# Splitting the context term of a recommendation tower into high and low halves on stacked rows: two fp32 passes replaced by one fp32r pass

## What is computed

```
def _cin_layer(X0, Xi, W, b):
    Wr = W.reshape(H, F0_, Fi)
    return jnp.einsum('hjk,bjd,bkd->bhd', Wr, X0, Xi) + b[None, :, None]
...
z = concatenate([X1.sum(2), X2.sum(2), X3.sum(2)], axis=1)       # 512 x 384
h = jnp.concatenate([z, dense_ctx], axis=1)                      # 512 x 400
h = jnp.maximum(h @ W_top1 + b_top1, 0.0)                        # 400 x 512
h = jnp.maximum(h @ W_top2 + b_top2, 0.0)                        # 512 x 256
y = h @ W_top3
```

## Time and profile before

| | |
|---|---|
| median of 3 runs | 665.23 us (664.14 to 666.54) |
| the profiled execution's own time | 665.45 us |
| its span | 663.6 us |
| PE busy | 648.5 us (98%) |
| DVE busy | 558.7 us (84%) |
| ACT busy | 440.8 us (66%) |
| POOL busy | 468.5 us (71%) |
| granted TensorE clock, mean | 0.992 of full speed |

### The profile page before, as it was taken

The page is one execution under the profiler, slowest core; times in us unless marked ns, Lnnn a source line. Parts: engine busy times, 40 slices in busy tenths (PEclk is TensorE's granted clock), DMA queues, the critical chain, the costliest instruction groups (busy, mean ns, idle before and its releaser), DMA issues.

```text
span 663.6 us, 11303 instructions
## 1 busy us (share of the span) xinstructions
PE 648.5 (98%) x3070; PEld 518.3 (78%) x3070; DVE 558.7 (84%) x1558; ACT 440.8 (66%) x1449; POOL 468.5 (71%) x376
## 2 busy tenths in 40 slices
PE   7998999999999999999999999999999999999997
PEld 7785678777788777777778877778778887777877
DVE  4669899999984799999995699999997589999970
ACT  3554667677763777777773677877785477778761
POOL 6888888888873688888875478787876367444540
PEclk8899999999999999999999999999999999999999
DMA  6013474140403004040311301313040300400000
GB/s 216 14 36 107 130 243 128 23 120 8 128 10 114 16 8 128 6 122 16 94 44 45 90 5 46 91 29 108 18 121 15 107 17 8 126 2 5 1 1 1
DMA packets 38357, 42.25 MB, mean 64 GB/s; under 512 B 17824, under 2 KB 22549, under 8 KB 38166
## 3 DMA queue, kind: packets, MB, share of 16 engines
q1 hardware_dynamic: 32661, 40.23, 19.9%
q0 software_dynamic: 5632, 1.31, 2.2%
HBM read 8.84 MB, written 0.00 MB: 13 GB/s over the span
## 4 chain that ended last, share of the span: by engine, by line
PE 92%; DVE 2%; DMA 2%; ACT 1%; issue 1%; POOL 1%; SPq 0%; POOLq 0%; DVEq 0%
PE p_u L804 22%; PE p_u L806 21%; PE p_u L805 21%; PE p_x L779 6%; PE p_tower L827 5%; PE p_g L818 5%; PE p_x L776 2%; PE p_x L774 2%; PE p_x L773 2%; PE p_tower L854 1%; DMA g_all<-w_in 1%; PE p_x L744 1%; DVE parts L636 1%; DVE z L595 1%; PE p_x L756 1%
## 5 line engine op out<-in xcount | busy, mean ns | idle before, releaser
L457 ACT ACTIVATE prod<-p_u,x0t 128x128 f32<-128x128 f32 x1024 | 290.4, 376 | 101.5 <-PE p_u L806 101.4
L636 DVE SCALAR_TENSOR_TENSOR parts<-p_u,x0t,parts 128x128 f32<-128x128 f32 x1024 | 283.4, 341 | 41.3 <-PE p_u L806 41.2
L804 PE MATMUL p_u<-w1h,x1h 128*128 128x512 f32 (+1 forms) x640 | 288.4, 451 | 1.0 <-ACT x1h L438 1.0
L806 PE MATMUL p_u<-w1h,x1l 128*128 128x512 f32 (+1 forms) x640 | 250.2, 391 | 0.0
L805 PE MATMUL p_u<-w1l,x1h 128*128 128x512 f32 (+1 forms) x640 | 250.1, 391 | 0.0
L335 POOL DMA_INDIRECT emb<-table_in,idx_all x176 | 207.9, 1181 | 49.9 <-issue 47.5
L354 POOL TENSOR_TENSOR parts<-parts,prod 128x512 f32<-128x512 f32 x128 | 176.2, 1377 | 51.7 <-ACT prod L457 38.3
L804 PEld LDWEIGHTS p_u<-w1h,x1h 128*128 128x128 f32 x640 | 120.9, 189 | 37.9 <-issue 8.6
L805 PEld LDWEIGHTS p_u<-w1l,x1h 128*128 128x128 f32 x640 | 121.5, 190 | 35.6 <-issue 10.8
L806 PEld LDWEIGHTS p_u<-w1h,x1l 128*128 128x128 f32 x640 | 120.7, 189 | 26.1
L349 POOL TENSOR_TENSOR parts<-prod 128x512 f32<-128x512 f32 x64 | 83.3, 1301 | 73.0 <-ACT prod L457 72.2
(11 more groups left out here) (86 smaller groups left out, 388.2 us busy)
## 6 DMA issues: line engine op xcount, KB each, us to landing
fac_b<-xx SPq DMA_DIRECT2D x90, 234.0 KB
fac_a<-xx SPq DMA_DIRECT2D x45, 78.0 KB
emb<-table_in,idx_all POOLq DMA_INDIRECT x176, 3.2
g_all<-w_in SPq DMA_DIRECT2D x3, 832.0 KB, 6.2
w<-w_in SPq DMA_DIRECT2D x1, 2496.0 KB, 9.2
xx<-xx SPq DMA_DIRECT2D x30, 78.0 KB
fac_b<-xx SPq DMA_DIRECT2D x15, 156.0 KB
bd<-x0t SPq DMA_DIRECT2D x120, 10.0 KB
```

Of the source, the lines that this page charges most:

```text
L457: last = nc.scalar.activation(dst[:, i * H:(i + 1) * H], u[:, i * H:(i + 1) * H], ACT.Copy, scale=x0t[:, par, t, j:j + 1])
L636: nc.vector.scalar_tensor_tensor(out=chain[i][:, p], in0=u[:, i * H:(i + 1) * H], scalar=x0t[:, par, t, j:j + 1], in1=add, op0=ALU.mult, o ...
L804: nc.tensor.matmul(u, xh, wh, start=True, stop=False)
L806: nc.tensor.matmul(u, xl, wh, start=False, stop=True).then_inc(u_full, 1)
```

## The change

The two context operands become fp32r tensors of 112 rows (`CTX_ROWS = 96 + CTX`). Rows 0, 32, 64 and 96 onward hold 16 rows each: for the weights `wt1c` high, high, low, low, and for the factors `ctxt` high, low, high, low. One matmul over the 112 rows then sums all four products of the halves; the rows between are zeros.

The raw fp32 rows are loaded elsewhere: the weights into `y_rows` (the row `y`, made 16 rows high) and the context into the first 16 rows of `h1`, which the tower first writes later. The four high halves are written by ACT (`context_high_half`) and the four low halves by DVE (`context_low_half`), 16 rows by 512 columns each, in slots 5, 7, 9 and 11 of macro batch 4 (`S_CTX`, `M == MACROS`). The low halves 0 and 2 wait for the high half of the same slot; 1 and 3 need only that of the slot before last. POOL is untouched; SP issues the same DMAs with one wait fewer, to other places.

```
+CTX_ROWS = 96 + CTX
+S_CTX = [5, 7, 9, 11]
+CTX_HIGH = [0, 32, 0, 64]
+CTX_LOW = [64, 96, 32, 96]
...
-        wt1c = sb("wt1c", [128, TOP1])
+        wt1c = sb("wt1c", [CTX_ROWS, TOP1], FP32R)
-        ctxt = sb("ctxt", [128, B])
+        ctxt = sb("ctxt", [CTX_ROWS, B], FP32R)
...
-        y = sb("y", [1, B])
+        y_rows = sb("y_rows", [CTX, B])
+        y = y_rows[0:1, :]
+        wt1c_raw = y_rows[:]
+        ctxt_raw = h1[0:CTX, :, :].rearrange("p c b -> p (c b)")
...
-                sp.wait_ge(context_cleared, 2)
-                sp.dma_start(wt1c[0:CTX, :], wt1_d[3 * 128:3 * 128 + CTX, :]).then_inc(tower_in, 16)
+                sp.dma_start(wt1c_raw, wt1_d[3 * 128:3 * 128 + CTX, :]).then_inc(context_in, 16)
...
+            def context_high_half(i):
+                raw, half = (wt1c_raw, wt1c) if i < 2 else (ctxt_raw, ctxt)
+                act.wait_ge(context_in, 16 * (2 + STACK))
+                act.wait_ge(context_cleared, 2)
+                nc.scalar.activation(half[CTX_HIGH[i]:CTX_HIGH[i] + CTX, :], raw, ACT.Copy).then_inc(context_high, 1)
...
             def tower_h1(n, p_h1):
                 act.wait_ge(h1_full, n + 1)
+                act.wait_ge(context_low, 4)
...
+                        if M == MACROS and s in S_CTX:
+                            context_high_half(S_CTX.index(s))
...
+            def context_low_half(i):
+                raw, half = (wt1c_raw, wt1c) if i < 2 else (ctxt_raw, ctxt)
+                high = 0
+                dve.wait_ge(context_high, 2 * (i // 2) + 1)
+                dve.wait_ge(context_in, 16 * (2 + STACK))
+                nc.vector.tensor_tensor(out=half[CTX_LOW[i]:CTX_LOW[i] + CTX, :], in0=raw,
+                                        in1=half[high:high + CTX, :].bitcast(FP32), op=ALU.subtract
+                                        ).then_inc(context_low, 1)
...
+                        if M == MACROS and s in S_CTX:
+                            context_low_half(S_CTX.index(s))
...
-                pe.wait_ge(tower_in, 16 * (4 + STACK))
+                pe.wait_ge(tower_in, 16 * 2)
+                pe.wait_ge(context_high, 4)
+                pe.wait_ge(context_low, 4)
```

More of the change, by code:

```diff
@@ L172, in build @@
         context_cleared = sem("context_cleared")
+        context_in = sem("context_in")
+        context_high = sem("context_high")
+        context_low = sem("context_low")
         idx_made = sem("idx_made")
@@ L292, in load_tower @@
                     n, at = FIRST_SAMPLES[c], GATHERS * c
-                    sp.dma_start(ctxt[0:CTX, c:MACRO_B:STACK], ctx_d[:, at:at + n], allow_slow_non_contiguous=True).then_inc(tower_in, 16)
-                sp.dma_start(ctxt[0:CTX, MACRO_B:B], ctx_d[:, MACRO_B:B]).then_inc(tower_in, 16)
+                    sp.dma_start(ctxt_raw[:, c:MACRO_B:STACK], ctx_d[:, at:at + n], allow_slow_non_contiguous=True).then_inc(context_in, 16)
+                sp.dma_start(ctxt_raw[:, MACRO_B:B], ctx_d[:, MACRO_B:B]).then_inc(context_in, 16)
             def body(n, has_prev, has_next):
@@ L692, in _ @@
             nc.vector.memset(bd[:], 0.0).then_inc(bd_cleared, 1)
-            nc.vector.memset(wt1c[:], 0.0).then_inc(context_cleared, 1)
-            nc.vector.memset(ctxt[:], 0.0).then_inc(context_cleared, 1)
+            nc.vector.memset(wt1c[:].bitcast(FP32), 0.0).then_inc(context_cleared, 1)
+            nc.vector.memset(ctxt[:].bitcast(FP32), 0.0).then_inc(context_cleared, 1)
             dve.wait_ge(w0_in, 16)
```

## The result

The changed kernel takes 671.56 us (median of 7 runs, 670.32 to 673.46) against 666.54 us (7 runs, 664.14 to 669.77) of the kernel before beside it: ratio 1.0088, 95% interval 1.0062 to 1.0114. It is slower, by 5.0 us in the medians and 5.9 us by the ratio, more than twice the 2.49 us that were forecast. The span of the profiled execution grew from 663.6 to 669.6 us.

What follows compares the result with a forecast made beforehand. PE bounds the kernel (busy 648.5 of 663.6 us), with a chain through a full DVE in macro batch 4. Delay 3.83 us minus 1.34 us gained gives +2.49 us: 667.7 us forecast against the median 665.23 us, range 665.3 to 669.3 us.

Steps and rivals of the forecast that it cites:

- the cost term of the sum: Macro batch 4: ACT's copy into g_all and PE's start of `tower_z3` come 3.30 + 0.53 = 3.83 us later.
- DVE is full ahead of the product of group 2: Macro batch 4, from slot 4 on: DVE runs back to back, first idle 0.93 us in slot 15.
- the chain behind it: Macro batch 4: product of group 2, z0h, quad, copy, `tower_z3`; any delay moves PE by its full length.
- The first low half waits for ACT, 0.41 us.: Slot 5 of macro batch 4: DVE, ready at 185.28 us, waits until 185.69 us for ACT's high half.
- Three low halves at 0.60 us, the fourth high half at 0.53 us.: Macro batch 4: DVE's three before the product add 1.80 us; ACT's one between z0h and slot 12's quad adds 0.53 us.
- POOL's collisions, 1.09 us.: Macro batch 4: POOL's additions lengthen the first two low halves by 0.72 and 0.37 us; the third meets none.
- The short pass costs one record.: Context matmuls of the towers: each single pass takes 0.112 us, not 0.223; twelve on the path gain 1.34 us.
- The bound of 0.06 us a pass: Context matmuls: fastest case for a short pass of 128 columns, raising the gain of twelve to 1.96 us.
- The 81 ns per matmul: Context matmuls: the skill's figure for 128 columns, giving 1.70 us gain; the prediction kept the trace's 0.112 us instead.
- The last block's passes give nothing.: Tail: its four short passes gain nothing, since PE waits 0.96 us for DVE's fold anyway.
- The prediction is wrong if `tower_z3` starts before 195 us.: Refuting sign in slot 15 of macro batch 4: PE's `tower_z3` starting before 195 us, against 192.26 us before the change.
- Or if PE is idle anywhere else that it was not: Refuting sign: new PE idle time outside the forecast waits, about 3.8 us in slots 10 to 15 of macro batch 4.

Runs made afterwards that it cites:

- e1: Changed kernel with all eight conversions in slots 15, 17, 19 and 21 of macro batch 4, not 5, 7, 9 and 11: 665.25 us, ratio 0.9997.
- e6: Changed kernel with only DVE's four low halves moved to slots 15, 17, 19 and 21, ACT's high halves left in place: 665.12 us, ratio 0.9993.
- e4: Changed kernel plus eight unread fp32r matmuls of 512 columns on PE before `tower_z3`'s wait in slot 15 of macro batch 4: 668.05 us, ratio 1.0052.
- e5: Changed kernel with DVE's low halves written to rows 0 to 15 of an unused tensor, products with low halves left out: ratio 1.0071.
- e11: Changed kernel plus eight unread fp32r matmuls before the slot 15 wait and five unread fp32 ones in the tail: 667.99 us, ratio 1.0029.

## Why the prediction was wrong

**The step that failed** is the cost term of the sum: "The copy, and PE's start of `tower_z3`, come 3.30 + 0.53 = 3.83 us later", taken as the whole cost. The delay itself was 4.56 us, and PE's clock behind the waits, of which the prediction has no word and which it thus put at nothing, cost another 1.54 us in macro batch 4 and 1.63 us in the tail of the profiled execution. The mechanism, its place and its sign were right. Point by point:

- *DVE is full ahead of the product of group 2 and the chain behind it has no slack.* Right: e1 moves the operations 10 slots on and the loss is gone, e6 splits it into DVE's part and ACT's.
- *The first low half waits for ACT, 0.41 us.* Near: 184.96 - 0.08 us, when DVE would have gone on, to 185.22 us, 0.34 us.
- *Three low halves at 0.60 us, the fourth high half at 0.53 us.* The durations were right (0.71 us for the third low half, which meets no addition of POOL, and 0.63 us), the distances too small: 0.11 us on each side of a low half, some 0.6 us for the three, and 0.12 us on each side of the high half. I took the distance from operations that keep their partitions and overlooked that these move 16 rows from partition 0 to 32, 64 or 96. The Trainium skill says it (VectorE: DVE Perf Modes, Two Vector instructions with no wait between them): an instruction whose output starts in another group of 32 partitions than the last output into the same memory did starts only when every earlier one has finished. The trace agrees for DVE (0.03 us behind the end, where 0.08 us ahead of it is usual), and shows the same on ACT, of which the page does not speak.
- *POOL's collisions, 1.09 us.* Right: 0.54 and 0.55 us behind POOL's end, on the first and the second low half, none on the third; 0.76 + 0.27 = 1.03 us.
- Together the chain was **4.6 us and not 3.83 us** (4.56 us by the start of `tower_z3`, 4.60 us by e4): 0.34 for the wait, 1.80, 1.03 for POOL, 0.6 for the holds on DVE, and 0.77 for the high half.
- *The short pass costs one record.* Right: 0.47 us for four of them, 1.41 us for twelve, where 1.34 us were forecast. The bound of 0.06 us a pass was not reached. The 81 ns per matmul of the Trainium skill (TensorE: Matmul & The Clock Gate, Back-to-back issue gap) would have given an estimated 1.70 us, which the trace does not show.
- *The last block's passes give nothing.* Worse: they lengthened PE's wait in the tail from 0.96 to 1.47 us, and the 1.63 us that were lost at half clock behind it were in no sum. That part is chance in half of the cases: e4, e5 and e6 have the same wait in their profiles and keep the clock.
- *The clock.* **1.54 us** in macro batch 4 (e4) and **1.63 us** in the tail of the profiled execution were missing. The forecast with the true chain, 4.6 - 1.4 = +3.2 us, would have been inside the range; the two stretches at 1.2 GHz carried the result out of it. The prediction had PE idle for 3.8 us between slots 10 and 15 (3.93 us measured) and priced only the idling. The trace of the kernel before has a warning that no row of the prediction shows: PE waits 1.22 and 0.54 us between 7.9 and 10.2 us, and from about 12 to 22 us it runs at half clock. The second of these windows is part of that; PE is busy in all of it:

```profile
8.00:10.00 2.00, 0.52 (x6) 0.38 (x6) 0.75 (x1) 0.23 (x2) 1.69 (x2) 1.00 0.16 17
14.00:16.00 2.00, 2.00 (x11) 1.85 (x9) 0.95 (x1) 1.45 (x2) 1.70 (x2) 0.50 1.00 415
```

Against it, the wait of 1.74 us at 56 us and the 0.96 us in the tail leave the clock at full. So the loss in macro batch 4 could be foreseen as a risk from that trace, and not as a certainty.

- *"The prediction is wrong if `tower_z3` starts before 195 us."* It started at 196.45 us. "Or if PE is idle anywhere else that it was not": it was idle in no new place, but 0.51 us longer in the tail.

## What to carry to other kernels

A cheap preparation is placed by the slack of the engine in that stretch and not by its average load: the same eight operations cost 6.1 us in slots 5 to 11 and nothing in slots 15 to 21. When a bound TensorE is made to wait, price the wait and what its clock may do behind it, and where a wait can't be avoided, unread matmuls in front of it can pay (1.54 and 1.52 us in macro batch 4 in the profiles of e4 and e11). Count the neighbours of an operation that writes to another group of 32 partitions, since both sides lose their overlap (0.11 us each here).

## What the runs showed that I had not expected

- PE waited 0.61, 0.91 and 2.41 us between 187 and 196 us, and TensorE then ran at 1.2 GHz until about 201 us: 1.54 us lost. In e5, with a last wait of 2.1 us, the clock stayed at full in the profiled execution; in the four profiles with 2.4 us it did not.
- Operations of ACT are held like those of DVE when their output starts in another group of 32 partitions: 0.66 instead of 0.53 us to the next one.
- The time to the start of macro batch 4 scatters by 3.7 us over the profiles, more than the whole gain of the change, and the granted clock of its first 40 us differs with it.
- 2 us of useless matmuls ahead of a wait made macro batch 4 1.5 us shorter in both profiles that have them.
